# Turning x for the application: fp16 parts and transposing DMAs in place of fp32 transposes on TensorE

## The reference, cut to what matters

```
k = conv(x, w1, 7x7, dilation 2, padding 6) + b1           # 256 -> 128
k = conv(k, w2, 1x1) + b2                                  # 128 -> 49
attn = softmax(k, axis=1)
x = sum over 49 taps (u, v) of attn[tap] * xp[:, :, 2u:2u+64, 2v:2v+64]
states: s = A @ s + Bvec, 64 steps;  yc = states @ Cmat
out = x + gelu(yc.T[None, :, None, :] + x * D)             # exact gelu
out = layernorm over channels(out) * ln_w + ln_b
```

## Time and profile before

| | us |
|---|---|
| median of 3 runs | 812.01 (809.2 to 813.11) |
| span of the profiled execution (the page gives no other time of it) | 807.6 |
| TensorE busy | 746.6, 92% |
| VectorE busy | 672.8, 83% |
| ScalarE busy | 562.8, 70% |
| GpSimd busy | 194.6, 24% |

### The profile page before, as it was taken

The page is one execution under the profiler, slowest core; times in us unless marked ns, Lnnn a source line. Parts: engine busy times, 40 slices in busy tenths (PEclk is TensorE's granted clock), DMA queues, the critical chain, the costliest instruction groups (busy, mean ns, idle before and its releaser), DMA issues.

```text
span 807.6 us, 27610 instructions
## 1 busy us (share of the span) xinstructions
PE 746.6 (92%) x12338; PEld 446.8 (55%) x12338; DVE 672.8 (83%) x867; ACT 562.8 (70%) x917; POOL 194.6 (24%) x115
## 2 busy tenths in 40 slices
PE   4969989998999999999999999999999999998994
PEld 2535544674557545764567545664567545764581
DVE  0898997988888988988888988988888988686775
ACT  2774454767786796867786696778786687488466
POOL 5114123024211243024211342114311441013011
PEclk9969999999999999999999999999999999999998
DMA  9472233023724147224704245324704230413124
GB/s 293 134 134 38 41 58 50 3 41 52 141 35 93 28 77 122 53 44 75 143 9 94 40 91 95 69 35 87 131 3 93 41 80 3 89 29 70 28 54 105
DMA packets 266721, 58.60 MB, mean 73 GB/s; under 512 B 266265, under 2 KB 266346, under 8 KB 266346
## 3 DMA queue, kind: packets, MB, share of 16 engines
q1 hardware_dynamic: 138488, 40.79, 23.9%
q10 hardware_dynamic: 128114, 16.04, 12.8%
HBM read 40.04 MB, written 16.78 MB: 70 GB/s over the span
## 4 chain that ended last, share of the span: by engine, by line
PE 35%; ACT 22%; DVE 16%; issue 9%; POOL 3%; ACTq 2%; DVEq 0%; POOLq 0%
PE cv L526 18%; PE wk L575 7%; ACT V L913 5%; ACT chs L967 4%; DVE V L1435 3%; PE wk L596 3%; PE wk L634 3%; POOL chs L411 2%; PE ms L606 2%; ACTq L957 2%; DVE o L1583 2%; ACT ms L1016 1%; DVE Z L1476 1%; DVE XT L1466 1%; DVE chs L1535 1%
## 5 line engine op out<-in xcount | busy, mean ns | idle before, releaser
L526 PE MATMUL cv<-V,W 128*32 128x496 f16 (+6 forms) x7840 | 428.9, 374 | 6.3 <-issue 4.1
L526 PEld LDWEIGHTS cv<-V,W 128*32 128x32 f16 (+1 forms) x7840 | 198.5, 96 | 204.8 <-issue 18.2
L913 ACT ACTIVATE V<-R,sc 128x1024 f16<-128x1024 f32 (+1 forms) x88 | 109.6, 1274 | 60.6 <-DVE R L1361 50.5
L386 POOL TENSOR_TENSOR R<-raw 128x1152 f32<-128x1152 f32 x32 | 95.2, 2976 | 201.5 <-DVE V L1435 102.4
L1435 DVE SCALAR_TENSOR_TENSOR V<-R,sc,V 128x1024 f16<-128x1024 f32 (+1 forms) x88 | 115.1, 1327 | 3.0 <-ACT V L913 3.0
L596 PE MATMUL wk<-band,XT 128*128 128x209 f16 (+1 forms) x1080 | 87.7, 238 | 3.3 <-ACT o L989 3.0
L596 PEld LDWEIGHTS wk<-band,XT 128*128 128x128 f16 x1080 | 78.7, 97 | 15.0 <-ACT o L989 8.5
L575 PEld LDWEIGHTS wk<-AT,sel 128*128 128x128 f16 x2268 | 69.6, 100 | 15.0 <-issue 8.6
L411 POOL TENSOR_TENSOR chs<-o 128x1024 f32<-128x1024 f32 x14 | 45.2, 3226 | 130.8 <-DVE o L1583 121.8
L575 PE MATMUL wk<-AT,sel 128*128 128x16 f16 (+1 forms) x2268 | 73.9, 190 | 0.1
L1361 DVE SCALAR_TENSOR_TENSOR R<-R 128x1024 f32<-128x1024 f32 (+1 forms) x56 | 68.6, 1257 | 0.0
(11 more groups left out here) (196 smaller groups left out, 931.1 us busy)
## 6 DMA issues: line engine op xcount, KB each, us to landing
raw<-in_x_dram SPq DMA_DIRECT2D x16, 1024.0 KB, 11.7
out_dram<-o SPq DMA_DIRECT2D x28, 512.0 KB, 4.3
AT<-in_x_dram ACTq DMA_DIRECT2D x82, 128.0 KB, 3.1
w1raw<-in_L_conv_w_dram SPq DMA_DIRECT2D x2, 3136.0 KB, 16.9
xs<-in_x_dram ACTq DMA_DIRECT2D x40, 128.0 KB, 3.0
out_dram<-o SPq DMA_DIRECT2D x8, 256.0 KB, 3.8
AT<-in_x_dram SPq DMA_DIRECT2D x4, 128.0 KB, 3.0
xs<-in_x_dram SPq DMA_DIRECT2D x2, 128.0 KB, 3.7
```

The costliest lines, as they stand in the source:

```text
L386: nc.gpsimd.tensor_tensor(R[buffer][:, :, :, :], rows_of(par, j + 2), rows_of(par, j), ALU.subtract).then_inc(pool_rows, 1)
L526: ins = pe.matmul(to.rearrange("p (w t c) -> p w t c", w=2, c=COLS)[:, :, :, c0:c1], W[:, ws, h * K7 + v, k0:k1], slot(n, a)[:, low, :, t0 ...
L913: nc.scalar.activation(v_array(n, a, 0), array(a), ACT.Identity, scale=sc[:, par, 3:4]).then_inc(vhi, 1)
```

## The change

`turn_x` leaves TensorE. ScalarE makes the high part straight from the fetched stage in SBUF (`x_high`), VectorE the low part (`x_low`), both into a new tile XS, which lies in the memory of `band`, with the two column parities pulled apart. Then SP issues one transposing DMA per stage, [128 partitions x 1024 fp16] to XT as eight 128x128 blocks (`turn_x` on SP). Waits that change: x_high of stage 0 waits until the application of m is done (y_done), band_high of stage 0 and apply wait for all eight transposing DMAs (xt_done, 16 each), and fetch_rows waits for xt_low of stage g - 3. In the order of SP the DMAs stand ahead of the stores and the raw load. next_load loses its wait for xt_done. In the first unit all eight stages move to the end of ScalarE's and VectorE's lists, with no low part before that. On VectorE x_low(n, par, 4) moves ahead of centre(m, 1, 0).

```diff
-        XT = sb("XT", [P, 2, TILES, HALVES, P], F16)
+        XT = sb("XT", [P, STAGES, 2, 2, HALVES, P], F16)
...
+        XS = band[:].rearrange("p l n r x -> p (l n r x)")[:, 0:STAGES * 4 * HALVES * P].rearrange(
+            "p (g l f) -> p g l f", g=STAGES, l=2)
+        columns_of = lambda k: stages[k % 3].rearrange("p (i c w) -> p w i c", c=TCOLS, w=2)
...
                 sp.wait_ge(pool_rows, POOL_ROWS * n)
-                sp.wait_ge(xt_done, 8 * n)
                 load(n + 1, 1 - par, b)
+
+            def turn_x(n, first, last):
+
+                for g in range(first, last):
+                    k = STAGES * n + g
+                    sp.wait_ge(xt_low, k + 1)
+                    sp.dma_start_transpose(XT[:, g].rearrange("p l w h c -> p (l w h) c"),
+                                           XS[:, g].rearrange("p l f -> p (l f)")).then_inc(xt_done, 16)
...
+            turn_x(0, 0, STAGES)
             for n in range(1, UNITS):
-                store(n, n % 2, (n - 1) // 2, 0)
+                b = (n - 1) // 2
+                turn_x(n, 0, 4)
+                store(n, n % 2, b, 0, 0)
+                turn_x(n, 4, STAGES)
+                store(n, n % 2, b, 0, 1)
                 if n < UNITS - 2:
                     next_load(n + 1, (n + 1) % 2, (n + 2) // 2)
-                store(n, n % 2, (n - 1) // 2, 1)
+                store(n, n % 2, b, 1, 0)
+                store(n, n % 2, b, 1, 1)
...
                 if y == 0:
                     pe.wait_ge(blo, 10 * m + 10)
+                    pe.wait_ge(xt_done, 16 * STAGES * (m + 1))
...
-            def turn_x(n, par, g, cold=False):
...
                 k = STAGES * n + g
                 if g < 3:
                     act.wait_ge(sel_done, STEPS * n)
-                    act.wait_ge(xt_done, STAGES * n)
-                else:
-                    act.wait_ge(xt_done, k - 2)
+                act.wait_ge(xt_low, k - 2)
                 for h in range(HALVES):
                     act.dma_start(stage(k)[:, h], tile_rows(n, g, h)).then_inc(xs_in[k % 3], 16)
 
-            def turned_x(n, par, g):
-                act.wait_ge(xt_done, 8 * n + g + 1)
-                nc.scalar.activation(XT[:, 0, 2 * g:2 * g + 2].rearrange("p t h c -> p (t h c)"), wk[:, g % 2, :],
+            def x_high(n, par, g):
+                k = STAGES * n + g
+                act.wait_ge(xs_in[k % 3], 32 * (k // 3) + 32)
+                if not g:
+                    act.wait_ge(y_done, 8 * n) if n else act.wait_ge(w_low, 2 * SETS)
+                nc.scalar.activation(XS[:, g, 0].rearrange("p (w i c) -> p w i c", w=2, c=TCOLS), columns_of(k),
                                      ACT.Identity, scale=sc[:, par, 3:4]).then_inc(xt_high, 1)
...
             def band_high(m, r):
+                if not r:
+                    act.wait_ge(xt_done, 16 * STAGES * (m + 1))
                 act.wait_ge(sel_done, 10 * m + r + 1)
...
-            def turned_x_low(n, par, g):
-                dve.wait_ge(xt_high, 8 * n + g + 1)
-                low, high = (XT[:, l, 2 * g:2 * g + 2].rearrange("p t h c -> p (t h c)") for l in (1, 0))
-                nc.vector.scalar_tensor_tensor(out=low, in0=wk[:, g % 2, :], scalar=sc[:, par, 3:4], in1=high,
+            def x_low(n, par, g):
+                k = STAGES * n + g
+                dve.wait_ge(xt_high, k + 1)
+                low, high = (XS[:, g, l].rearrange("p (w i c) -> p w i c", w=2, c=TCOLS) for l in (1, 0))
+                nc.vector.scalar_tensor_tensor(out=low, in0=columns_of(k), scalar=sc[:, par, 3:4], in1=high,
                                                op0=ALU.mult, op1=ALU.subtract).then_inc(xt_low, 1)
```

More of the change, by code:

```diff
@@ L340, in load, with store @@
                     sp.dma_start(raw[par][:, h, PAD:PAD + ROWS, :], xv[b, par, h]).then_inc(raw_in[par], 16)
[L342 to L346, removed]
+            def store(n, par, b, q, h):
+                sp.wait_ge(affine, 4 * (n - 1) + 2 * q + h + 1)
+                sp.dma_start(ov[b, 1 - par, h, :, 16 * q:16 * q + 16, :], o[:, q, h]).then_inc(o_free, 16)
             def next_load(n, par, b):
                 sp.wait_ge(pool_rows, POOL_ROWS * n)
-                sp.wait_ge(xt_done, 8 * n)
                 load(n + 1, 1 - par, b)
+            def turn_x(n, first, last):
[4 more added lines that the diff above has]
+                                           XS[:, g].rearrange("p l f -> p (l f)")).then_inc(xt_done, 16)
             sp.dma_start(w2raw[:, :], w2.rearrange("k m a b -> k (m a b)")).then_inc(s_w2, 16)
@@ L540, in turn_logits @@
                     pe.wait_ge(z_step, ZSTEPS * m + ZSTEPS)
-                    pe.wait_ge(xt_low, 8 * m + 8)
+                    if m:
+                        pe.wait_ge(xs_made, 8 * m)
                 else:
@@ L595, in apply @@
                         for k, (xl, bl) in enumerate(((0, 0), (1, 0), (0, 1))):
-                            ins = pe.matmul(to, XT[:, xl, 2 * (XTILES * j + e) + w, h, :],
+                            ins = pe.matmul(to, XT[:, XTILES * j + e, xl, w, h, :],
                                             band[:, bl, XROWS * w + j, r0 - TROWS * j + PAD:r1 - TROWS * j + PAD,
@@ L1091, in unit @@
                 gelu(m, 1, 1)
-                turned_x(n, par, 0)
+                x_high(n, par, 0)
                 fetch_rows(n, 3)
                 square(m, 0, 0)
-                turned_x(n, par, 1)
+                x_high(n, par, 1)
                 fetch_rows(n, 4)
                 square(m, 0, 1)
-                turned_x(n, par, 2)
+                x_high(n, par, 2)
                 fetch_rows(n, 5)
                 inverse_deviation(m, 0)
-                turned_x(n, par, 3)
+                x_high(n, par, 3)
                 fetch_rows(n, 6)
@@ L1105, in unit @@
                 scale_shift(m, 0, 0)
-                turned_x(n, par, 4)
+                x_high(n, par, 4)
                 fetch_rows(n, 7)
@@ L1109, in unit @@
                 table_of_ln()
-                turned_x(n, par, 5)
+                x_high(n, par, 5)
                 square(m, 1, 0)
                 square(m, 1, 1)
-                turned_x(n, par, 6)
-                turned_x(n, par, 7)
+                x_high(n, par, 6)
+                x_high(n, par, 7)
                 scale_shift(m, 0, 1)
@@ L1236, in _ @@
             v_high(0, 0, 5)
-            turned_x(0, 0, 0)
-            fetch_rows(0, 3)
             weights_high(8, 10)
             sum_1(0, 0)
-            turned_x(0, 0, 1)
-            fetch_rows(0, 4)
             v_high(0, 0, 6)
@@ L1245, in _ @@
             v_high(0, 0, 8)
-            turned_x(0, 0, 2)
-            fetch_rows(0, 5)
             v_high(0, 0, 9)
             weights_high(10, 11)
-            turned_x(0, 0, 3)
-            fetch_rows(0, 6)
             sum_2(0, 0)
@@ L1255, in _ @@
             weights_high(12, 13)
-            turned_x(0, 0, 4)
-            fetch_rows(0, 7)
-            turned_x(0, 0, 5)
             bound(1, 1, 0)
@@ L1262, in _ @@
             v_high(1, 1, 1)
-            turned_x(0, 0, 6)
-            turned_x(0, 0, 7)
+            x_high(0, 0, 0)
+            fetch_rows(0, 3)
+            x_high(0, 0, 1)
+            fetch_rows(0, 4)
+            x_high(0, 0, 2)
+            fetch_rows(0, 5)
+            x_high(0, 0, 3)
+            fetch_rows(0, 6)
+            x_high(0, 0, 4)
+            fetch_rows(0, 7)
+            x_high(0, 0, 5)
+            x_high(0, 0, 6)
+            x_high(0, 0, 7)
             act.wait_ge(late_cleared, 3)
@@ L1663, in unit @@
                 centre(m, 0, 1)
-                turned_x_low(n, par, 0)
+                x_low(n, par, 0)
                 if nxt:
                     make_y1_plus(n + 1)
-                turned_x_low(n, par, 1)
+                x_low(n, par, 1)
                 logits_rows(n, False)
@@ L1671, in unit @@
                 logits_d(n, par)
-                turned_x_low(n, par, 2)
+                x_low(n, par, 2)
                 normalise(m, 0, 0)
                 normalise(m, 0, 1)
-                turned_x_low(n, par, 3)
+                x_low(n, par, 3)
                 if nxt:
@@ L1678, in unit @@
                     v_low(n + 1, other, 1)
+                x_low(n, par, 4)
                 centre(m, 1, 0)
                 centre(m, 1, 1)
[L1681 to L1684, removed]
+                x_low(n, par, 5)
+                x_low(n, par, 6)
+                x_low(n, par, 7)
             def product_maxima():
@@ L1828, in _ @@
             weights_low(5, 6)
-            turned_x_low(0, 0, 0)
             make_y2_plus(0)
@@ L1834, in _ @@
             make_y2_minus(0)
-            turned_x_low(0, 0, 1)
             weights_low(6, 7)
@@ L1845, in _ @@
             v_low(0, 0, 8)
-            turned_x_low(0, 0, 2)
             weights_low(10, 11)
             make_q1(0)
-            turned_x_low(0, 0, 3)
             logits_2(0, 0)
@@ L1862, in _ @@
             make_y1_minus(1)
-            turned_x_low(0, 0, 4)
             logits_rows(0, True)
```

(11 more changed lines are left out.)

16 lines of the change are left out of this document (removed).

## The result

The changed kernel takes 933.2 us (932.3 to 936.7, 4 runs) against 811.4 in the same comparison: 1.152 times as long, 95% interval 1.149 to 1.156. The forecast was 907, range 835 to 1000. The profiled span is 930.7, 123.1 more than before. Measured from one turn of the attention to the next, a steady unit grew from 89.6 to 105.8 us.

What follows compares the result with a forecast made beforehand. Bound: the hand-over ring between engines, especially the ScalarE-VectorE chain, not TensorE's 92% busy time. Middle units 66.6 + last 8 + first 11 + clock 9 = 94.6 us, on 812.0 gives 907 us; range 835 to 1000.

Steps and rivals of the forecast that it cites:

- The five waits: ScalarE's queue, fetch_rows: five fetches wait for VectorE's low part, then issue; 11.1 us a unit, bounds 2.8 to 15.
- The third wait: ScalarE's fetch behind x_low(2), with 1.5 us added for GpSimd on a logit step; normalising 6.2 us late.
- the fifth fetch: ScalarE's fetch behind x_low(4): 1.0 us to issue, so spread_mean(1) starts 11.5 us late.
- the exchange "one for one": ScalarE's and VectorE's passes over x read SBUF instead of PSUM: 0 to 0.5 us a unit gained, taken as 0.
- The clock: TensorE's stop ahead of variance(1) lowers its clock: 0.9 for variance, 0.4 for turns, 1.3 us a unit, 9 in all.
- TensorE's freed time at 0: Transposes of x leave TensorE, 5.29 us a unit, but it only reaches its waits earlier: gain 0.
- The transposing DMAs at 0: SP's queue: eight per unit, 3.8 us each; up to 6.1 us each they cost nothing.
- a sign of being wrong: Listed check on SP's queue: a transposing DMA over 6 us would show the forecast wrong.
- First unit: Eight low parts in a row at the end of the lists, in lockstep with fetches: +11 us.
- six middle units: Steady units, each lengthened 11.1 us by ScalarE's held queue: 66.6 us, clock term counted apart.
- the last and the tail: Unit n = 7, without v_high(n+1, 1) and low parts behind it: about 8 us, clock term counted apart.

Runs made afterwards that it cites:

- before_fetch_waits_low: Kernel before, TensorE's transposes kept: from the second unit fetch_rows waits for VectorE's low part, low part 4 moved ahead; 897.3 us, ratio 1.108.
- fetch_on_sp: Changed kernel with the fetches of stages 3 to 7 issued by SP ahead of each transposing DMA, not by ScalarE; 863.1 us, ratio 1.064.
- psum_low: Changed kernel whose low part, from the second unit on, reads a resting PSUM bank times 0 in place of x in SBUF; 906.9 us.
- before_cheap_turn: Kernel before, from the second unit on one fp16 matmul in place of each stage's four fp32 transposes; 806.7 us, ratio 0.996.
- spare_transposes: Changed kernel with four unread fp32 transposes of the identity put back on TensorE at the old places in seven units; 934.3 us, ratio 1.153.
- few_turning_dmas: Changed kernel issuing, after the first unit, only the last of each unit's eight transposing DMAs; 933.8 us.
- fetch_on_sp_psum_low: Changed kernel with fetches 3 to 7 issued by SP and low parts reading a resting PSUM bank from the second unit on; 847.2 us, ratio 1.047.

## Why the prediction was right, step by step

**The five waits.** This was the step that carried the forecast, and its first four rows came out within 0.9 us of where they were put. With mean(0) at 361.58 before and 511.38 after as common zero (149.80 us apart), and the forecast of the last row with the clock's 1.3 us in it:

| step | before | forecast | after, less 149.80 |
|---|---|---|---|
| square(0,0) | 367.98 | 370.8 | 370.55 |
| square(0,1) | 369.51 | 374.2 | 374.17 |
| normalising | 378.71 | 384.9 | 384.94 |
| spread_mean(1) | 382.33 | 393.8 | 394.67 |
| turn_logits(0) | 392.72 | 403.8 | 406.43 |
| turn_attention | 412.22 | 424.6 | 428.30 |

The third wait was right in size by luck in part. I had put 1.5 us of GpSimd on a logit step ahead of low part 2; the logit steps took 0.68 and 0.74 us, and low part 2 itself took 2.26 in place of 0.75, the same 1.5. (My terms also add up to 378.6 for its end, where I wrote 378.2.)

before_fetch_waits_low and fetch_on_sp show the cause from both sides: put in alone, the wait costs 88 us, and taken out it gives back 70.

**What was too small** is at the end of the table. turn_logits(0) is 2.6 us later than forecast: the fifth fetch took 1.64 us to issue in place of 1.0, and low part 6 met GpSimd and took 2.31 in place of 0.7. The term behind it is the exchange "one for one", which I had put at 0. The pass that moved from PSUM to SBUF takes 0.75 us alone and not 0.68, and up to 2.3 beside GpSimd, where with its operand in PSUM it never went over 0.752. psum_low prices that at 26 us, where I had 1.5 us a unit, some 10 us. The Trainium skill had the rule, in SBUF — State Buffer (SBUF: two separate sides): a VectorE instruction with two SBUF inputs and a GpSimd instruction that reads SBUF exclude each other for a whole instruction. The 56 passes with a PSUM operand agree, and so do the low parts that end 0.5 us behind GpSimd's sum.

**The clock**: 1.3 us a unit forecast, 2.4 measured (turn_attention is 16.1 us later than before and turn_logits(0) 13.7). I had priced variance (0.9) and the turns (0.4). Variance(1)'s 0.9 cost nothing, as TensorE then waited 1.61 us for VectorE. turn_logits(0) lost 0.9, and I had left out the 40 matmuls behind it, 4.11 in place of 2.35 us at a granted clock of 0.54.

**TensorE's freed time at 0**: right. 3 of some 16 to 20 us in before_cheap_turn, and nothing measurable of 37 in spare_transposes.

**The transposing DMAs at 0**: right. They land in 4.3 us by the median (I took 3.8), and SP is held 1.23 us for one issue. The longest landed in 7.3, over the 6 us that I had named as a sign of being wrong, and few_turning_dmas shows that even so they cost nothing. The engine time that queue q1 gained is 30.3% of 930.7 less 23.9% of 807.6, 89 us over 64 DMAs, 1.4 us of all 16 engines each. By the Trainium skill's two figures, in DMA: Bandwidth & Descriptors (Latency and other measured facts) and in VectorE: DVE Perf Modes (The three transpose paths), 256 KB were an estimated 1.0 and 10.5 us. The 1.4 us of engine time is near the first, and eight squares landing in 4.3 us don't fit the second, taken one after another.

**The sum.** First unit +11.6 to its turn of the attention (143.16 to 154.75; forecast 11), six middle units +97.5 (154.75 to 789.68, less 143.16 to 680.55; forecast 74.4), the last and the tail +14.0 (forecast 9.3). The 28 us short are the middle units' and the last's, 3.9 and 4.7 each. The first unit is near by two errors that cancel: its last low part ends at 130.3 where I had 132.2 and before it was 121.1, so the row of low parts cost 9.2 and not 11, and the other 2.4 are the clock (0.59 from 132 to 139.9 us), for which I had no term there.

**What stays open.** fetch_on_sp_psum_low is at 847 without the queue waits and without these collisions. Its unit of 93.4 is 3.8 above before. Of its 36.7 us of span over the kernel before, 11.1 are the first unit and 23 the six middle ones. In one of these (342.18 to 435.28, 93.1 us) high part 7 waits 1.99 us for its fetch to land, and from turn_logits(0) to the turn of the attention it takes 1.4 us longer than before, with turn_logits(0) at 1.65 us in place of 1.09. So late fetches and the clock are seen in it, but no run takes them apart.

## What to carry to other kernels

A wait placed ahead of a DMA issue on a compute engine's queue is a wait of everything behind it on that engine: five such waits held ScalarE 1.9 to 4.4 us each in a unit, issue included. Before moving work off the busiest engine, ask what the hand-over chain between the others does, and put such issues on a queue whose next instruction waits for the same event anyway. An operand that moves from PSUM to SBUF is not the same pass: look whether GpSimd works beside it.

## What the runs showed that I had not expected

- A VectorE pass with a single SBUF input (tensor_scalar, fp32 at a step of two to fp16) was 0.48 us, and still went up to 2.05 beside GpSimd.
- GpSimd loses as well: a sum of 2.4 us took 4.79.
- A transposing DMA of 256 KB from SBUF to SBUF is 1056 packets, holds SP for 1.23 us and lands in 4.3 (2.7 to 7.3).
- Useless TensorE work made a kernel 5 us faster (860.6 to 855.5), with a granted clock of 0.98 in place of 0.95 in the middle.
